# Order of work on VectorE, ScalarE and GpSimd inside the attention slots of a macaron block

## What is computed

```python
x = x + 0.5 * ffn(layernorm(x))          # 8 experts, top 2, rank 16
x = x + attn(layernorm(x))               # below; 32 heads, 4 sequences of 512
x = x + 0.5 * ffn(layernorm(x))

# attn, for one sequence
q = rms_norm(x @ wq_a.T, q_norm_w) @ wq_b.T            # 128 plain + 64 rotated per head
kv_c, k_pe = split(x @ wkv_a.T)                         # latent of 128, rotated key of 64
k_nope, v = split(rms_norm(kv_c, kv_norm_w) @ wkv_b.T)  # 128 + 128 per head
scores = (q_nope @ k_nope.T + rope(q_pe) @ rope(k_pe).T) / sqrt(192)
probs = softmax(causal(scores))
out = (probs @ v) @ wo.T
```

## Time and profile before

| | us |
|---|---|
| median of 3 runs (2349.46 to 2356.67) | 2350.86 |
| the profiled execution | 2356.33 |
| its span in the trace | 2354.5 |
| one pass of `body`, first pair (load to load, 851.59 to 917.01) | 65.4 |

### The profile page before, as it was taken

One profiled execution on the slowest core, in us unless ns is written; L12 is line 12 of the kernel. 1 busy time (PEld: TensorE's weight loads), 2 busy tenths in 40 slices (PEclk: granted clock), 3 DMA queues, 4 the chain that ended last, 5 costly groups with the idle time before them and its releaser, 6 DMA issues.

```text
span 2354.5 us, 44541 instructions
## 1 busy us (share of the span) xinstructions
PE 2181.5 (93%) x11548; PEld 1815.1 (77%) x11548; DVE 1611.1 (68%) x3415; ACT 1371.7 (58%) x3561; POOL 1257.2 (53%) x1643
## 2 busy tenths in 40 slices
PE   8979999999999999999889979999999999999988
PEld 7957777777777777777778957888888888887877
DVE  7646667666766666767777646666666666666677
ACT  6545566656665566665666545555555555555553
POOL 5325565666656656566554345555555555555543
PEclk9989999999999999999999989999999999999999
DMA  4024433333344343433424133333333333333321
GB/s 164 14 60 127 135 130 131 114 99 88 126 135 130 126 135 128 133 110 118 159 97 142 28 110 107 106 106 106 106 106 106 106 106 106 106 106 107 104 92 72
DMA packets 217104, 258.01 MB, mean 110 GB/s; under 512 B 145616, under 2 KB 174416, under 8 KB 214992
## 3 DMA queue, kind: packets, MB, share of 16 engines
q1 hardware_dynamic: 212432, 244.64, 33.6%
q10 hardware_dynamic: 4608, 12.58, 1.6%
HBM read 127.14 MB, written 79.69 MB: 88 GB/s over the span
## 4 chain that ended last, share of the span: by engine, by line
PE 52%; DVE 12%; DMA 11%; issue 8%; ACT 7%; POOL 7%; SPq 3%; POOLq 0%; DVEq 0%; ACTq 0%
PE ps L861 39%; DMA stage<-in_wo 8%; PE ps L940 4%; DVE xacc L2184 4%; DVE arena L1837 3%; ACT arena L1383 3%; PE ps L1224 2%; PE ps L1168 2%; DMA arena<-arena 2%; PE ps L887 1%; SPq L756 1%; DVE negmax L2163 1%; DVE ps L2161 1%; ACT stage L1683 1%; PE ps L875 1%
## 5 line engine op out<-in xcount | busy, mean ns | idle before, releaser
L2184 DVE TENSOR_TENSOR xacc<-ps,xacc 128x512 f32<-128x512 f32 x896 | 602.8, 686 | 280.8 <-PE ps L861 267.4
L1837 DVE TENSOR_TENSOR arena<-ps,arena 128x512 fp32r<-128x512 f32 (+4 forms) x744 | 428.8, 578 | 326.3 <-ACT arena L1383 325.3
L861 PE MATMUL ps<-arena,extra 128*128 128x512 f32 x1920 | 540.0, 410 | 70.4 <-DVE xacc L2184 67.6
L861 PEld LDWEIGHTS ps<-arena,extra 128*128 128x128 f32 x1920 | 338.2, 188 | 190.1 <-DVE xacc L2184 114.9
L1683 ACT ACTIVATE stage<-ps,negmax 128x128 f32<-128x128 f32 (+6 forms) x512 | 261.3, 510 | 381.3 <-DVE negmax L2163 376.4
L861 PE MATMUL ps<-zT,arena 128*128 128x512 f32 (+1 forms) x1746 | 451.1, 403 | 10.3 <-ACT stage L1383 7.0
L1383 ACT ACTIVATE arena<-ps 128x512 fp32r<-128x512 f32 (+4 forms) x744 | 360.0, 506 | 115.4 <-PE ps L861 50.4
L2468 POOL TENSOR_TENSOR extra<-extra_plain,extra 128x256 fp32r<-128x256 f32 (+1 forms) x256 | 224.9, 879 | 320.4 <-ACT extra L1383 319.7
L861 PEld LDWEIGHTS ps<-zT,arena 128*128 128x128 f32 x1746 | 320.1, 191 | 80.6 <-ACT stage L1383 10.6
L861 PE MATMUL ps<-arena 128*128 128x512 f32 x960 | 262.6, 410 | 30.5 <-POOL arena L2468 24.3
L1692 ACT ACTIVATE stage<-stage,rrec 128x128 f32<-128x128 f32 (+6 forms) x512 | 235.8, 532 | 71.0 <-DVE rrec L2169 71.0
(11 more groups left out here) (129 smaller groups left out, 3159.2 us busy)
## 6 DMA issues: line engine op xcount, KB each, us to landing
kept_b<-arena SPq DMA_DIRECT2D x16, 3584.0 KB, 11.0
arena<-kept_b SPq DMA_DIRECT2D x112, 512.0 KB, 5.6
arena<-arena SPq DMA_DIRECT2D x128, 128.0 KB, 3.0
stage<-in_wo SPq DMA_DIRECT2D x16, 1024.0 KB, 13.1
stage<-stage SPq DMA_DIRECT2D x248, 64.0 KB, 2.0
extra<-arena SPq DMA_DIRECT2D x120, 128.0 KB, 3.0
kept_q<-arena SPq DMA_DIRECT2D x16, 768.0 KB, 4.1
arena<-kept_q ACTq DMA_DIRECT2D x32, 384.0 KB, 6.2
```

The lines of the kernel that those rows point to most:

```text
L861: last = nc.tensor.matmul(dst, w, m, start=start and n == 0, stop=stop and n == len(passes) - 1, skip_group_check=skip)
L1837: return nc.vector.tensor_tensor(dst, src, part.bitcast(F32), ALU.subtract)
L2184: nc.vector.tensor_tensor(xs, bank_y(k, j), xs, ALU.add).then_inc(y_added, 1)
```

## The change

TensorE's and SyncE's programs stay the same, row for row. No arithmetic is added or taken away. The order on three engines moves, in `body` alone:

- ScalarE, `k` = 2 of the first pair: `split_a(m, 1)` and `split_a(m, 2)` go ahead of the first two exponentials, and the high parts of T3, T4 and B22 go between the others.
- ScalarE, `k` = 1 of the first pair: `split_a(m, 2)` ahead of `turned(3)`; `valued` between the third and the fourth of `norms`.
- ScalarE, `k` = 0 and 2 of the second pair: `split_a(m, 1)` ahead of the second exponential, `split_a(m, 2)` ahead of `turned(3)`.
- VectorE, `k` = 0 and 2 of the second pair: the second maximum ahead of the second low part; additions 2 and 3 ahead of `pt_split(3)` and `maxima(3)`.
- VectorE, `k` = 2 of the first pair: additions 2 and 3 ahead of `maxima(3)`.
- VectorE, `k` = 1 of the first pair: addition 4 ahead of `second_row`.
- GpSimd, `k` = 2 of the first pair: the sum s3 ahead of the first low part.

```diff
-            def norms(p, g, k):
+            def norms(p, g, k, first=0, end=NS):
...
-            def valued(n, used=0):
+            def valued(n, used=0, whole=True):
...
-                split_a(n, 0)
+                if whole:
+                    split_a(n, 0)
...
+                    if k == 2 and p == 0:
                         turned(n, before, 0)
+                        split_a(m, 1)
+                        turned(n, before, 1)
                         exps(p, g, k, 0)
+                        split_a(m, 2)
+                        fills(k, "output")
+                        split_b(g, T3, last)
+                        turned(n, before, 2)
                         exps(p, g, k, 1)
+                        split_b(g, T4, last)
+                        turned(n, before, 3)
+                        exps(p, g, k, 2)
+                        split_b(g, B22, last)
+                        exps(p, g, k, 3)
+                    elif k == 1 and p == 0:
...
+                        turned(n, before, 2)
+                        split_a(m, 2)
+                        turned(n, before, 3)
+                        exps(p, g, k, 2)
...
+                        norms(p, g, k, 0, 3)
+                        valued(n, whole=False)
+                        norms(p, g, k, 3)
+                        split_a(n, 0)
+                        continue
+                    elif k % 2 == 0 and p:
+                        turned(n, before, 0)
+                        exps(p, g, k, 0)
+                        turned(n, before, 1)
+                        split_a(m, 1)
+                        exps(p, g, k, 1)
+                        fills(k, "output")
+                        turned(n, before, 2)
+                        split_a(m, 2)
+                        turned(n, before, 3)
+                        exps(p, g, k, 2)
+                        exps(p, g, k, 3)
...
+                if b22:
+                    pt_split(n, before, 3)
+                    adds(2, 3)
+                    maxima(p, g, k, 3)
+                elif k % 2 == 0 and p:
+                    adds(2, 3)
+                    pt_split(n, before, 3)
+                    maxima(p, g, k, 3)
...
+                adds(4)
                 if k == 1 and p == 0:
                     second_row(g, ev, False)
-                adds(4)
...
-                split(0)
+                if not all_first:
+                    split(0)
                 G.tensor_tensor(s3, a22, a21, ALU.subtract).then_inc(o_sum, 1)
+                if all_first:
+                    split(0)
```

More of the change, by code:

```diff
@@ L2228, in slot @@
                     maxima(p, g, k, 1)
-                fills("front")
-                pt_split(n, before, 0)
-                pt_split(n, before, 1)
-                if k % 2 == 0:
+                    fills("front")
+                    pt_split(n, before, 0)
+                    pt_split(n, before, 1)
+                elif b22:
+                    pt_split(n, before, 0)
+                    pt_split(n, before, 1)
                     maxima(p, g, k, 1)
+                else:
+                    pt_split(n, before, 0)
+                    maxima(p, g, k, 1)
+                    pt_split(n, before, 1)
                 fills("output")
@@ L2237, in slot @@
                 adds(0, 1)
-                pt_split(n, before, 3)
-                fills("second")
-                maxima(p, g, k, 3)
-                adds(2, 3)
+                if b22:
[6 more added lines that the diff above has]
+                    maxima(p, g, k, 3)
+                else:
+                    pt_split(n, before, 3)
+                    fills("second")
+                    maxima(p, g, k, 3)
+                    adds(2, 3)
                 if k == 1 and p == 0:
```

59 lines of the change are left out of this document (32 added, 27 removed).

## The result

The changed kernel takes **2242.63 us** (median of 4 runs, 2241.34 to 2245.74), the kernel before beside it 2352.35 (4 runs, 2349.46 to 2356.67): a ratio of 0.953, 95% interval 0.9515 to 0.9553. That is 110 us less, where 88 were forecast. 2263 was too slow by 20 us, and 2243 to 2300 misses the result by 0.4 us at its low end; the nearest case was rival 2, "more than the sum", at 2237. The profiled execution took 2245.74 us, with a span of 2243.9; against 2356.33 before that is 110.6 us.

What follows compares the result with a forecast made beforehand. TensorE, busy 93% of the span, was taken as the bound, with the loop of the load also limiting first-pair passes. Second pair 39 plus first pair 49 gave 88 us off the median 2350.86: 2263 us, range 2243 to 2300.

Steps and rivals of the forecast that it cites:

- rival 2: More than the sum: thin margins hold, the load's loop gives 4.2 too, B11 is free; 2237 us, chance 0.1.
- Second pair: Even slots: earlier second maximum and additions gain 1.4 us in each of thirty, 42 us, taken as 39.
- thin margins: Second pair, even slots: `pt_split(3)` ready 0.2 us before `values`, addition 4 ready 0.35 us before output 6.
- (a): First pair, slot 1: output 6 no longer waits for addition 4 behind `second_row`; gain 1.2 us.
- (b): First pair, slot 2: ScalarE's first exponential comes later, so scores 2 wait for their bank; loss 0.6 us.
- (c): First pair, slot 2, scores 2 to `values`: small waits for additions 2 and 3 and T3 go; gain 1.35 us.
- (d): First pair, slot 3: GpSimd's work moves forward 3.6 us, so output 0 doesn't wait; gain 1.45 us.
- (e): First pair, start of each pass: TensorE's wait for the load and the slower start behind it; gain 0.8 us.
- the loop of the load: First pair: rotation, product write, then weights' load; a pass can't be shorter than this loop, which gains 3.6 us by (d).
- row against the sum: VectorE's low parts of B11 and B22 differ, 1.76 and 1.01 us; B11 free gives 11 us more, B22 hit 4 less.
- what costs nothing: First pair, slot 1: `split_a(m, 2)` delays the third exponential 0.5 us harmlessly; GpSimd's T sums start a microsecond earlier.
- Rivals 1, 3, 4 and 5: 1: GpSimd gains half, 2285, 0.2; 3: late last maximum, 2297, 0.12; 4: ScalarE late, 2372, 0.04; 5: waits renamed, 2350, 0.04.

Runs made afterwards that it cites:

- Experiments 3 and 4: Changed kernel's second pair: 3 puts additions 2 and 3 back behind the last maximum, 2260.6 us; 4 puts ScalarE's order and the second maximum back, 2264.8 us.
- experiment 8: Changed kernel with slot 1's `split_a(m, 2)` back behind the third exponential and GpSimd's sum of T3 behind the low parts of T2 and T1: 2259.1 us.
- experiment 5: Changed kernel with slot 2 of the first pair back in the old order on ScalarE, VectorE and GpSimd, slot 1 kept new: 2302.0 us.
- Experiment 7: Changed kernel with `split_a(m, 2)` of slot 1 in the first pair put back behind the third exponential: 2255.8 us.
- Experiments 6 and 11: Changed kernel, slot 1 of the first pair: 6 puts addition 4 back behind `second_row`, 2266.7 us; 11 puts product `m3` ahead of scores 1 on TensorE, 2236.8 us.

## Why the prediction was right or wrong

**Second pair: right, step by step.** Forecast 39; measured 38.7 in the trace and 39.4 alone. Gain per even slot 1.4: it is 1.40 in the slot shown (7.96 to 6.56), up to the values. The waits for additions are under 10 us (2.4), both thin margins held: the values at 1548.72 and output 6 at 1551.22 start without a wait. The low part of tile 3 ended at 1548.44, 0.28 ahead of the values, where 0.2 were foreseen. Experiments 3 and 4 show both halves of the reasoning, each with half of the gain. That the sum fits so well is in part luck. The 3 us were taken off for margins, which held; but a whole group is only 2.51 shorter (57.96 to 55.45), 1.26 an even slot and not 1.4. Of that, 0.09 is seen in the slot shown: the values to output 6 take 2.50 and not 2.41 once nothing waits ahead of them. The rest isn't traced.

**First pair, TensorE's path: the sum nearly right (4.66 for 4.2), one term wrong in sign.** From start to start, one pass:

| stretch on TensorE | before | after | won | forecast |
|---|---|---|---|---|
| `m0` to output 6 of slot 1 (a) | 25.96 | 24.58 | 1.38 | 1.2 |
| to scores 2 of slot 2 (b) | 4.25 | 4.15 | 0.10 | -0.6 |
| to the values (c) | 8.32 | 6.91 | 1.41 | 1.35 |
| to output 0 of slot 3 (d) | 9.93 | 8.40 | 1.53 | 1.45 |
| to the next `m0`, the load's wait (e) | 16.95 | 16.71 | 0.24 | 0.8 |
| pass | 65.41 | 60.75 | 4.66 | 4.2 |

(a), (c) and (d) stand. (b) didn't come: scores 2 start at 968.45 with no wait, since the norms of slot 1 ended earlier than assumed and took ScalarE's whole queue with them. (e) is smaller, since most of the load's wait is still there. The two misses, 0.7 and -0.56, nearly cancel.

**The step that failed is the loop of the load, 3.6 a pass**, taken as a bound apart from TensorE's path and made from (d) alone. The pass got 4.66 shorter. Two errors are in the step. Its stretches, from the load's issue (851.59 before, 926.61 after):

| stretch on GpSimd | before | after | won | forecast |
|---|---|---|---|---|
| load to sums of slot 2 | 40.18 | 38.83 | 1.35 | 0 |
| to the low parts of T3 and T4 | 7.97 | 4.78 | 3.19 | 3.6 |
| to the end of the rotation | 10.31 | 10.15 | 0.16 | 0 |
| to the next load | 6.96 | 7.01 | -0.05 | 0 |
| pass | 65.42 | 60.77 | 4.65 | 3.6 |

The second line is (d), and it is a little smaller than forecast. The first is what the prediction waved through: "`norms` end no earlier, so (a) doesn't reach ScalarE", and the earlier `valued` "only makes the operands ready 0.7 sooner". These are rows of before for the first line: VectorE's reciprocal, right behind the low part of B11, GpSimd (sum of T3, sums of slot 2) and ScalarE (high parts of T2 and T1, norms, then `valued`):

```profile
888.62 0.16 DVE L2169 RECIPROCAL rrec<-rowsum 128x4 f32<-128x4 f32 x1
```

```profile
886.85 1.30 POOL L2503 TENSOR_TENSOR stage<-stage 128x512 f32<-128x512 f32 x1
...
891.77 0.46 POOL L2472 TENSOR_TENSOR extra_plain<-extra_plain,arena_plain 128x128 f32<-128x128 f32 x1 [0.69 <-ACT extra_plain L1383]
```

```profile
886.93 1.15 ACT L1383 ACTIVATE arena<-stage 128x512 fp32r<-128x512 f32 x2 [0.29 <-POOL stage L2501]
...
888.82 2.24 ACT L1692 ACTIVATE stage<-stage,rrec 128x320 f32<-128x320 f32 x4 [0.26 <-DVE rrec L2169]
890.97 0.36 ACT L1383 ACTIVATE arena_plain<-ps 128x256 f32<-128x256 f32 x1
```

and of after, ScalarE (the same) and GpSimd (sum of T3, low parts of T2 and T1, sums of slot 2):

```profile
961.58 1.14 ACT L1383 ACTIVATE arena<-stage 128x512 fp32r<-128x512 f32 x2
...
963.10 1.62 ACT L1692 ACTIVATE stage<-stage,rrec 128x320 f32<-128x320 f32 x3
964.62 0.37 ACT L1383 ACTIVATE arena_plain<-ps 128x256 f32<-128x256 f32 x1
```

```profile
960.63 1.28 POOL L2561 TENSOR_TENSOR stage<-stage 128x512 f32<-128x512 f32 x1
962.37 2.71 POOL L2567 TENSOR_TENSOR arena<-stage,arena 128x512 fp32r<-128x512 f32 x2 [0.46 <-ACT arena L1383]
965.44 0.46 POOL L2527 TENSOR_TENSOR extra_plain<-extra_plain,arena_plain 128x128 f32<-128x128 f32 x1 [0.35 <-ACT extra_plain L1383]
```

Before, GpSimd's sums of slot 2 waited 0.69 us for `valued`; so `valued` was in the loop, and was in sight in the trace of before. It stands behind the norms, and these behind two things: the reciprocal, which stands behind the low part of B11, and the high parts of T2 and T1 in ScalarE's own order. Counted from the load's issue, the norms start at 888.82 - 851.59 = 37.23 before and 963.10 - 926.61 = 36.49 after, 0.74 earlier. B11 itself starts at the same point of the pass (35.35 and 35.37), so TensorE's path doesn't explain it. About half is the stall of B11, which is gone: with B11 free but T sums late (experiment 8) the norms start at 36.83, 0.40 earlier than before. The other 0.34 is on ScalarE: before (0.29) and in experiment 8 it waits for GpSimd's T sum ahead of the high part of T2, now it doesn't. Both come from GpSimd's earlier T sums. `valued` comes a further 0.62 earlier, one norm (four took 2.24, three 1.62). 0.74 + 0.62 = 1.36, the 1.35 of the first line. That the edits of slot 1 make this line is shown by experiment 5 (38.78); its division is read from the traces, and no kernel here changes one of its parts alone.

GpSimd itself had to be earlier too: before, it was idle for only 0.69 ahead of these sums, so without its earlier T sums it could have used only that much of the 1.35. Experiment 7, which puts the T sums back, loses 0.69.

The second error is the form of the bound: the pass was taken as the shorter of two gains, 4.2 and 3.6, as if the loop of the load were a thing apart. Experiments 6 and 11 show that it runs through TensorE's own work, so that what TensorE gains there (output 6 of slot 1, `q2`) shortens it too, while the load's wait stays about as it is (6.3 and 6.5 us in 14).

**B11 and B22, the "row against the sum".** The prediction left 1.76 and 1.01 as they were and named plus 11 us if B11 came free. It did, and B22 too. The rows of three kernels fit one reading. Before, B11 starts at 886.94, in the middle of GpSimd's sum, which ends at 888.11 to 888.15, and it ends at 888.70. In experiment 7 it starts at 908.91, GpSimd's sum ends at 910.06 to 910.09, it ends at 910.65. B22 before: starts at 901.80, GpSimd's low parts end at 902.26, it ends at 902.81. In the changed kernel the sum ends at 961.91, B11 starts at 961.98 in GpSimd's idle time and takes 0.68. Where the low part started inside a GpSimd instruction it was through 0.6 us after that one's end. The Trainium skill, "SBUF — State Buffer" ("Who interferes with whom"), says that a VectorE instruction with two SBUF inputs and a GpSimd instruction that reads SBUF exclude each other, and that the second to start waits for the whole of the first. Here the traces agree: 0.6 us behind the other's end is nearly the 0.68 that the low part takes alone. It is `split_a(m, 2)` in slot 1, listed under what costs nothing, that does this: it brings GpSimd's T sums 1.2 us forward and out of B11's way (experiment 7 puts it back, and B11 takes 1.74). The contention doesn't vanish altogether: the third rotation pass now takes 1.60 (1.30 elsewhere), in the time of B22 (975.57), which keeps its 0.69.

**The signs foreseen.** A pass of 61.8: it is 60.8. Waits of output 6 in slot 1 and output 0 in slot 3 gone: yes. A new wait ahead of scores 2 of slot 2: no. The load's wait still there: yes, at 0.43, read as the sign that the loop is the bound; but experiment 11 shows the wait to stay while the pass shrinks with TensorE's work, so the sign doesn't separate the two. The swap DMAs were foreseen just in time for the second rotation pass; GpSimd's gap ahead of it is 0.34 and for its own first pass, so they were. Rivals 1, 3, 4 and 5 did not happen: counted from TensorE's `m0`, GpSimd's slot 3 sums are 4.73 us earlier (40.65 and 45.38), no output 6 waits in the passes shown, no slot is longer, and the waits went with the time. Of rival 2 the margins, the gain of the loop and B11 came true, and at 2237 it was 6 us too fast. It had a chance of 0.1 and was cut off by the range's low end. That chance was too small: B11's row showed a stall that a shift of GpSimd by the microsecond foreseen would end, and the shift was part of the change.

## What to carry to other kernels

Where each period waits for a transfer, follow the loop back through every engine before bounding the gain by it: it may run through the bounding engine's own work, and then what that engine gains shortens the loop too. When an instruction takes much longer than others of its shape, look at what the other engine ran when it started, price the reorder with and without that stall, and follow what is queued behind it. Moving a transfer forward in a queue pays only if no wait in that queue then holds back what others need.

## What the runs showed of the hardware

- A VectorE low part of 128x512 with both inputs from SBUF took 0.68 us alone, 1.01, 1.74 and 1.76 where GpSimd was in an instruction when it started, and ended 0.6 us behind the end of GpSimd's each time. GpSimd's 128x512 instructions went from 1.28 to 1.60 and 1.75.
- TensorE's lost time is more than its idle time: 0.47 and 0.43 us of idle gave 0.75 and 0.69 a pass when taken away.
- The load of 1024 KB took 13.1 us behind the writing of 3584 KB, and 6.8 to 6.9 ahead of it; the writing took 11.0 us ahead and 14.7 to 15.0 behind.
